# Second token tile's load ahead of the last weight block, q's fourth product two places up at loop entry, and the last pair's token groups earlier

## The reference, cut to what matters

```python
x = L0_attn_hidden_states                                   # 4 x 256 tokens, width 512
x = x + 0.5 * _L0_ffn_ref(_layernorm(x), A, B, Wr)          # 64 experts of rank 16, top 16 by score
x = x + _L0_attn_ref(_layernorm(x), wq, wkv, wo)            # 32 heads of 128, causal
x = x + 0.5 * _L0_ffn_ref(_layernorm(x), A, B, Wr)
...
scores = jnp.einsum('bqhd,bkhd->bhqk', q[..., :DN], k) * scale
probs = jax.nn.softmax(scores, axis=-1)
attn = jnp.einsum('bhqk,bkhd->bqhd', probs, v).reshape(B, S, H * DV)
return jnp.einsum('bse,ed->bsd', attn, wo)
```

## Time and profile before

| | |
|---|---|
| time of three runs | 1036.54 us median (1036.46 to 1036.55) |
| profiled execution | 1036.7 us, its span 1034.7 us |
| PE | busy 1023.6 us, 99% of the span |
| DVE | 687.5 us, 66% |
| ACT | 554.0 us, 54% |
| POOL | 533.4 us, 52% |
| granted TensorE clock | 1.000 over the span |
| DMA | 168.17 MB, mean 163 GB/s |

### The profile page before, as it was taken

One profiled execution on the slowest core, in us unless ns is written; L12 is line 12 of the kernel. 1 busy time (PEld: TensorE's weight loads), 2 busy tenths in 40 slices (PEclk: granted clock), 3 DMA queues, 4 the chain that ended last, 5 costly groups with the idle time before them and its releaser, 6 DMA issues.

```text
span 1034.7 us, 18708 instructions
## 1 busy us (share of the span) xinstructions
PE 1023.6 (99%) x5588; PEld 888.9 (86%) x5588; DVE 687.5 (66%) x1815; ACT 554.0 (54%) x1480; POOL 533.4 (52%) x473
## 2 busy tenths in 40 slices
PE   8999999999999999999999999999999999999998
PEld 7999888888888888888888888888878888889997
DVE  6778852432467766767776766776787988766553
ACT  4112455555367676667666667666776566531110
POOL 5431378996189777779777788777420000000000
PEclk9999999999999999999999999999999999999999
DMA  9700254772734444453444444443568878840000
GB/s 365 321 0 1 82 203 183 264 265 93 254 92 134 146 144 127 152 155 140 138 145 133 144 158 145 133 148 130 168 251 322 310 240 291 288 159 11 21 20 31
DMA packets 83704, 168.17 MB, mean 163 GB/s; under 512 B 8528, under 2 KB 24912, under 8 KB 82640
## 3 DMA queue, kind: packets, MB, share of 16 engines
q1 hardware_dynamic: 83664, 167.68, 47.2%
HBM read 102.37 MB, written 63.44 MB: 160 GB/s over the span
## 4 chain that ended last, share of the span: by engine, by line
PE 94%; DVE 3%; ACT 1%; POOL 1%; DMA 1%; issue 0%; POOLq 0%
PE bank L276 28%; PE bank L278 28%; PE bank L277 27%; PE bank L565 4%; PE bank L554 3%; PE bank L583 3%; PE bank L332 1%; PE bank L284 1%; DMA o_raw<-keep_o 0%; PE bank L359 0%; POOL wq_lo L1329 0%; PE bank L542 0%; DVE prob L1103 0%; DMA x<-x_in 0%; DVE upT_lo L1953 0%
## 5 line engine op out<-in xcount | busy, mean ns | idle before, releaser
L1320 POOL TENSOR_SCALAR ve<-mv 128x1 f32<-128x1 f32 x24 | 6.3, 264 | 306.6 <-DVE mv L976 306.3
L680 ACT ACTIVATE bank<-bank,nmax 128x128 f32<-128x128 f32 (+1 forms) x256 | 105.6, 453 | 4.4 <-DVE nmax L1090 4.4
L1103 DVE TENSOR_SCALAR prob<-bank,rinv 128x128 f32<-128x128 f32 (+1 forms) x256 | 95.1, 414 | 4.6
L276 PE MATMUL bank<-xc_lo,wq_hi 128*128 128x512 f32 x224 | 91.7, 410 | 0.4 <-POOL wq_lo L1329 0.4
L1090 DVE CUSTOM_DVE_ANT_0 bank<-bank,mask 128x128 f32<-128x128 f32 (+1 forms) x256 | 83.5, 389 | 11.4 <-PE bank L278 11.4
L276 PE MATMUL bank<-o_lo,ow_hi 128*128 128x512 f32 x224 | 88.9, 397 | 2.1 <-DVE o_lo L969 2.1
L634 ACT CAST o_hi<-o_raw 128x1024 fp32r<-128x1024 f32 x56 | 59.2, 1057 | 55.1 <-DMA o_raw<-keep_o 48.4
L276 PE MATMUL bank<-xc_lo,wk_hi 128*128 128x512 f32 x224 | 88.7, 396 | 0.0
L278 PE MATMUL bank<-xc_hi,wq_hi 128*128 128x512 f32 x224 | 87.9, 393 | 0.0
L278 PE MATMUL bank<-xc_hi,wk_hi 128*128 128x512 f32 x224 | 87.6, 391 | 0.0
L278 PE MATMUL bank<-o_hi,ow_hi 128*128 128x512 f32 x224 | 87.4, 390 | 0.0
(11 more groups left out here) (168 smaller groups left out, 3148.7 us busy)
## 6 DMA issues: line engine op xcount, KB each, us to landing
o_raw<-keep_o SPq DMA_DIRECT2D x49, 512.0 KB, 4.3
keep_v<-out_hl SPq DMA_DIRECT2D x64, 256.0 KB, 2.3
v<-keep_v SPq DMA_DIRECT2D x64, 256.0 KB, 3.5
keep_o<-att_comb SPq DMA_DIRECT2D x60, 256.0 KB, 2.3
keep_o<-att SPq DMA_DIRECT2D x45, 256.0 KB, 3.1
stage_v<-wv SPq DMA_DIRECT2D x4, 2048.0 KB, 9.1
stage_wq<-wqk SPq DMA_DIRECT2D x16, 512.0 KB, 3.3
keep_vraw<-out_raw SPq DMA_DIRECT2D x64, 128.0 KB, 2.1
```

The source lines that it names most:

```text
L276: nc.tensor.matmul(dst, a_hi, b_lo, start=first, stop=False, skip_group_check=onto)
L680: nc.scalar.activation(sp[b][:, a:e], sp[b][:, a:e], ACT.Exp, bias=nmax[:, c:c + 1], scale=-1.0, accum_out=rsum[:, c:c + 1]).then_inc(s["e ...
L1103: nc.vector.tensor_scalar(prob[:, b, a:e], sp[b][:, a:e], rinv[:, c:c + 1], None, ALU.mult).then_inc(s["p_ready"], 1)
```

## The change

Three places. At the start, tile 1 is loaded ahead of the fourth weight block, and on DVE its statistics stand ahead of the third low part and its scaling ahead of the fourth. At loop entry, q's fourth product moves ahead of k's seventh and fifth. In the last pair, group 1's load waits for q's last product instead of k's (group 2's waits for k's now), ACT rounds group 2 ahead of the copy of the attended unit 0, and DVE does the even group ahead of the maximum.

```diff
@@ act_pair @@
                     if j == 0:
                         act_o_tokens(act, 1)
                         act_o_weight(act, 1)
+                        act_o_tokens(act, 2)
...
                 act_attended(act, p, j)
                 if final:
-                    if j < 3:
+                    if j in (1, 2):
                         act_o_tokens(act, 2 * j + 2)
@@ dve_pair @@
                 if final:
                     if j < 3:
                         dve_o_weight(dve, j + 1)
+                        dve_o_tokens(dve, 2 * j + 2)
...
                 if j < 2 or not final:
                     dve_softmax_max(dve, u + 2, j)
                 if final:
-                    if j < 3:
-                        dve_o_tokens(dve, 2 * j + 2)
+                    pass
@@ load_tokens @@
             if m >= O_SLOTS:
                 sp_.wait_ge(s["o_used"], m - O_SLOTS + 1)
-            elif m == 1:
-                sp_.wait_ge(s["kx_ready"], 4 * PAIRS)
+            elif m in (1, 2):
+                sp_.wait_ge(s["qx_ready" if m == 1 else "kx_ready"], 4 * PAIRS)
@@ block.sync @@
             for k in range(KD):
+                if k == KD - 1:
+                    sync.dma_start(x[:, 1, :], x_in[1]).then_inc(s["x1_loaded"], 16)
                 sync.dma_start(upT_raw[:, k, :], up_w[:, k, :]).then_inc(up_loaded[k], 16)
-            sync.dma_start(x[:, 1, :], x_in[1]).then_inc(s["x1_loaded"], 16)
@@ block.tensor @@
             pe_scores(pe, 0, 0)
+            pe_m4(pe, "q", 0)
             pe_m7(pe, "k", 0)
             pe_m5(pe, "k", 0)
-            pe_m4(pe, "q", 0)
             pe_m4(pe, "k", 0)
@@ block.vector @@
             for k in range(1, KD):
+                if k == KD - 2:
+                    dve.wait_ge(s["x1_loaded"], 16)
+                    dve_stats(dve, 1, 0, x[:, 1, :])
+                elif k == KD - 1:
+                    dve_normalise(dve, 1, 0, x[:, 1, :])
                 dve.wait_ge(s["up_hi"], k + 2)
                 nc.vector.tensor_tensor(upT_lo[:, k, :], upT_raw[:, k, :], upT_hi[:, k, :].bitcast(F32),
                                         ALU.subtract).then_inc(s["up_split"], 1)
-                if k == KD - 2:
-                    dve.wait_ge(s["x1_loaded"], 16)
-                    dve_stats(dve, 1, 0, x[:, 1, :])
-            dve_normalise(dve, 1, 0, x[:, 1, :])
```

## The result

The changed kernel takes 1035.63 us (median of 22 runs, 1034.23 to 1036.49), the kernel before 1036.57 (22 runs, 1035.9 to 1038.36): ratio 0.9988 [0.9983, 0.9994], 0.94 us less, with 0.6 to 1.8 in the interval.

A forecast was written before the change was run, and what follows sets the result against it. PE was taken as the bound, busy 1023.6 of 1034.7 us. Gains of 0.2 (start), 0.6 (loop entry) and 0.4 (last pair) sum to 1.2 us, from 1036.54 to 1035.3 us; range 1034.2 to 1036.4.

The forecast's parts named there:

- The bound and the waits: Whole kernel: 11 us of idle PE in all; four PE gaps at the changed places, together 4.4 us, are the ceiling.
- The start: First tiles: transposes lose their wait, but POOL's down-weight low parts are held by DVE's fourth low part; gain 0.2 us.
- One of my signs of being wrong: At the start: the forecast is wrong if POOL's `downT_lo` starts before DVE's fourth low part ends.
- The wait for `upT_lo` before the fourth block: At the start: sign of being right, PE's fourth block waits for `upT_lo` near 15.2.
- One cover: Load order at the start: the fourth block lands about half a block later, but DVE wants it only at 13.9.
- Loop entry: Before pair 1: q's fourth product 2.7 us earlier lets POOL's split end near 287.9, removing the `wq_lo` wait; gain 0.6 us.
- The last pair: Output projection groups 1 to 6: 1.66 us won at group 2, but the later maximum leaves 0.4 at group 6.
- The new wait before group 6: Last pair on PE: sign of being right, a new wait of about 0.6 us for `o_lo` before group 6.
- first rival: Last pair keeps what it gains at group 2, 1.3 to 1.7 us there; total 2.4 to 2.7, 1034.0 us; chance 0.11.
- The sum: Whole kernel: start 0.2, loop entry 0.6 and last pair 0.4 make 1.2 us, giving 1035.3 us.
- the gains add: Behind each gap: work is released by PE or engines PE releases, so gains at one place carry to the next.
- The slower rival: At the start, POOL's low part starts before DVE's fourth and holds it, PE's fourth block 2.1 us late; 1037.6 us; chance 0.06.

The follow-up runs named there:

- start_only: Kernel before with only the start's part: tile 1 loaded ahead of the fourth weight block, its statistics and scaling one low part earlier; 1036.37 us, ratio 0.9999.
- s3_after: Changed kernel with one VectorE subtraction of the output projection (`s3`, 1.1 us) moved from group 13 to behind group 7; 1035.66 us, ratio 0.9994.
- after_again: The changed kernel measured once more, unaltered, on another chip; 1036.09 us, ratio 0.9992 against the kernel before.
- sp_early: Changed kernel with the weight pieces of groups 7 and 8 issued ahead of group 7's tokens; 1035.54 us, ratio 0.9989.
- load_only: Kernel before with only the conditions on which groups 1 and 2 are loaded in the last pair changed; 1036.26 us, ratio 0.9993.
- order_only: Kernel before with only the last pair's moves on ACT and DVE, loads issued as before; 1037.11 us, ratio 1.0.
- the light pair: Kernel before and changed kernel, each with four output projection weight pieces loaded beside groups 17 to 20 instead of earlier; 1037.07 and 1035.85 us.
- s3x2: Changed kernel with two VectorE weight differences moved up, one behind group 7, the next ahead of group 13; 1035.72 us, ratio 0.9989.
- entry_only: Kernel before with only q's fourth product moved up at loop entry; 1036.18 us, ratio 0.9996.

## Why the prediction was right

- **The bound and the waits.** The gaps named were the right ones. I had written that a measurement tells about 0.2% from none; the 22 runs told 0.09% from none.
- **The start: 0.2, measured 0.21 and 0.22.** The transposes wait no more, and the down projection is at 24.06 + 0.34 = 24.40, where 24.4 was said. The fourth block starts at 14.94 + 0.34 = 15.28 (15.2 said). The reason, POOL held by DVE's fourth low part, is shown by start_only's pair of rows; without the hold I had estimated 0.5. The Trainium skill, "SBUF — State Buffer", section "Who interferes with whom", by which whichever of the two issues first blocks the other fully, fits these rows. Some things in this step were not as written:
  - Two small errors cancel in the 0.2: `hT_lo` and the down projection lie 0.84 apart before (23.77 and 24.61), so the reckoned 23.67 gives 24.51, a gain of 0.1; `hT_lo` came at 23.23 + 0.34 = 23.57, because POOL's three low parts took 6.98 us from the end of the hold and not 7.10. That tenth is luck.
  - One of my signs of being wrong did appear: POOL's `downT_lo` is shown as started at 14.35, before DVE's fourth low part ended at 14.84. The sign was badly chosen, since a held instruction is shown as started, as `ve` was in the earlier trace rows; what tells a hold is when it ends.
  - The wait for `upT_lo` before the fourth block is missing in the change's own profile, whose third block ran late at half the clock, and is there in start_only and five others; in s3_after, at the full clock, the third block began at 12.68 + 0.10 = 12.78 (12.8 said) and the transposes at 14.26 + 0.10 = 14.36 (14.3).
  - One cover was thinner than I wrote: the fourth block was rounded at 11.93 instead of 10.58, with the shift 1.7 us later and not half a block's time, and its rounding ended at 13.03, 0.53 before DVE took it. In the other traces with this edit its rounding began anywhere from 10.22 to 12.06.
  - The gain is not safe: in after_again and sp_early DVE's second low part began 0.6 to 0.8 us later than in the change's profile (9.68 and 9.89 against 9.09), released by landings, and at 24.61 these two were 0.39 and 0.61 later against their own first row, not 0.2 earlier. The other six with this edit were 0.19 to 0.22 earlier. The edit need not be the cause: load_only, which has the old start, was 0.29 later in the same way.
- **Loop entry: 0.6, measured 0.67 and 0.66.** The split ended at 283.87 + 3.52 + 0.57 = 287.96 on the clock of before (287.9 said).
- **The last pair: 0.4, measured 0.43 and 0.44.** Net of the shift at 759.65 group 1 was 0.41 earlier (0.4 said), group 2 1.63 (1.66), group 6 0.43 (0.39), and the second exponential, 777.32 against 779.08, 0.40 (0.39). The new wait before group 6 is 0.36, 0.52 with the modelled end (0.6 said). load_only and order_only show that the chain was read rightly: all of the gain is from the load, and of the 0.4 about 0.1 belongs to the trace before. That the wait at group 2 would keep its gain (first rival) is refuted by order_only.
- **The sum: 1.2, measured 0.94.** The interval holds 1.2, so the times show no term to be wrong. If one was, it is none of the three but the sentence that what PE gains is carried on, "the gains add". They add up to group 6; behind it lies a stretch in which landings, and DVE's full row behind them, set the pace, and I had not costed it. By the table that is 0.2 us, not told from nothing, and 1.2 less 0.2 is near the median. Whether it is 0 or 0.4 stays open: the interval of the time (0.6 to 1.8 us) holds both, after_again's 0.75 speaks for the larger and the light pair's 1.22 for the smaller.
- **The slower rival** didn't come: DVE's fourth low part started first in every trace that I read there, 0.16 to 0.79 us ahead of POOL's step. In five of the eight traces with this edit the two were released by the same scaling and 0.16 or 0.17 us apart; in the change, start_only and both POOL came later because ACT's `downT_hi` released it. No run shows what would happen in the other order.

## What to carry to other kernels

Follow a wait that is removed to the next place where the engine waits: the largest wait on PE, 1.6 us, was worth nothing, and a load issued earlier that left this wait as it was gave 0.3 to 0.4. An instruction that is held by another engine is shown as started and long; look at where it ends. For gains below 1 us compare marks ahead of and behind the edit inside one trace, because the end of a single trace here moved by up to 1 us on landings alone. An early start into a stretch where DMA is full can be taken back by landings; look at that stretch before adding gains up.

## What the runs showed of the hardware

TensorE's granted clock was not full near 9 to 12 us in most traces, of kernels in which PE's program is the same to there. After, in columns as above (granted clock third from the end):

```profile
9.00:10.00 1.00, 0.96 (x3) 0.96 (x4) 0.91 (x1) 0.90 (x2) 0.00 (x0) 0.50 1.07 369
10.00:11.00 1.00, 1.00 (x6) 1.00 (x5) 0.99 (x2) 0.27 (x1) 0.00 (x0) 0.50 0.85 247
11.00:12.00 1.00, 1.00 (x5) 1.00 (x5) 0.98 (x2) 0.07 (x1) 0.70 (x1) 0.50 1.01 414
```

That is 1.2 GHz in place of 2.4. Of the 13 kernels above 11 had such a stretch, s3_after and s3x2 had none, nor had the trace before; PE had had matmuls since 1 us, with a pause of 1.40 us just before the first block at 8.16. It costs little here, since PE has a pause of its own a little later: start_only, with the dip, and s3_after, without, show the same net 0.2 us at 24.61.

A POOL instruction that came while DVE ran one with two operands in SBUF was held to its end: `ve`, 0.19 us at 21.90, took 1.14 at 11.30, and the three low parts took 7.47 or 8.00 us by how early they came, with the same end (21.82 and 21.84). The other way round, DVE's gate instruction took 1.62 us at 17.93 and 0.23 at 25.97.

DMA with full queues moved 332 to 412 GB/s in the stretches of 4 us shown here, and a lead of the issue passed on to a landing anywhere between nearly all and hardly: against before, group 13 came 0.22 to 1.17 us earlier in four traces whose group 6 was 1.26 to 1.79 earlier (the change, after_again, s3_after and s3x2), and 1.44 earlier in entry_only, where group 6 was 1.57 earlier.
